# Feed-forward pipeline of a two-layer decoder: transposes moved from TensorE to VectorE and DMAs

## The reference

```
x = layernorm(x + local_attention(x) @ Wo.T + bo)
x = layernorm(x + cross_attention(x, ctx))
# blocks of 16: scale = max|x|/6, rounded to the grid 0, .5, 1, 1.5, 2, 3, 4, 6
gate = q(x) @ q(w_gate).T          # 512 -> 1408
up   = q(x) @ q(w_up).T
h    = silu(gate) * up
x = layernorm(x + q(h) @ q(w_down).T)   # 1408 -> 512
```

## Time and profile before

| | |
|---|---|
| median of 3 runs | 2977.15 us (2976.79 to 2977.43) |
| the profiled execution | 2972.92 us, span 2971.2 us |
| mean granted clock of TensorE | 0.963 |
| PE busy | 2687.5 us, 90% |
| VectorE busy | 1836.1 us, 62% |
| ScalarE busy | 863.2 us, 29% |
| last stage | from about 1728 us to the end |

### The profile page before, as it was taken

How to read it: one execution, slowest core, us unless ns; L and a number is a source line. 1 busy time by engine, 2 the same in 40 slices (tenths; PEclk the granted TensorE clock), 3 DMA queues, 4 the chain that set the end, 5 groups by cost and what they waited for, 6 DMA issues and landing times. The chain is left out here.

```text
span 2971.2 us, 39571 instructions
## 1 busy us (share of the span) xinstructions
PE 2687.5 (90%) x14548; PEld 1389.4 (47%) x14548; DVE 1836.1 (62%) x3454; ACT 863.2 (29%) x1356; POOL 769.2 (26%) x791
## 2 busy tenths in 40 slices
PE   8999588999996999578887859999999999999997
PEld 4444255555553455244444524444444444444443
DVE  4787403666675344277777736777777777777664
ACT  1111122333322333267767601222222222222210
POOL 1232003544552333355555410000000000000000
PEclk9999699999998999799999979999999999999999
DMA  4332510000000233322222420000000000000000
GB/s 169 128 124 86 156 62 1 1 1 1 1 1 32 79 105 98 91 62 79 83 78 80 143 95 11 15 15 14 15 15 15 15 15 15 15 15 15 11 8 11
DMA packets 172110, 146.36 MB, mean 49 GB/s; under 512 B 23784, under 2 KB 136424, under 8 KB 170896
## 3 DMA queue, kind: packets, MB, share of 16 engines
q1 hardware_dynamic: 158264, 131.58, 14.0%
q10 hardware_dynamic: 13656, 12.26, 1.3%
HBM read 91.29 MB, written 52.43 MB: 48 GB/s over the span
## 5 line engine op out<-in xcount | busy, mean ns | idle before, releaser
L2062 PE MATMUL bank<-tiles,tl_HT 128*128 128x512 f32 x704 | 321.4, 598 | 10.6 <-ACT tl_HT L2120 10.6
L2038 PE MATMUL bank<-tiles,tl_XQT 128*128 128x512 f32 (+1 forms) x768 | 322.2, 563 | 0.0
L2043 PE MATMUL bank<-tiles,tl_XQT 128*128 128x512 f32 (+1 forms) x768 | 318.0, 557 | 0.0
L2248 DVE TENSOR_TENSOR tl_HQ<-bank,tl_HQ 128x512 f32<-128x512 f32 (+1 forms) x96 | 62.1, 647 | 282.5 <-PE bank L2043 282.5
L1556 POOL TENSOR_SCALAR_AFFINE_SELECT tiles<-tiles 128x512 f32<-128x512 f32 x256 | 171.3, 673 | 233.4 <-ACT tiles L1729 189.8
L2043 PEld LDWEIGHTS bank<-tiles,tl_XQT 128*128 128x128 f32 x768 | 145.9, 190 | 156.4 <-issue 122.4
L2038 PEld LDWEIGHTS bank<-tiles,tl_XQT 128*128 128x128 f32 x768 | 142.5, 192 | 136.0 <-issue 110.5
L2105 ACT ACTIVATE tl_HQ<-bank 128x512 f32<-128x512 f32 (+1 forms) x96 | 53.9, 562 | 511.2 <-PE bank L2038 511.2
L2062 PEld LDWEIGHTS bank<-tiles,tl_HT 128*128 128x128 f32 x704 | 126.9, 191 | 141.6 <-issue 141.6
L1978 POOL TENSOR_TENSOR tl_rs<-tl_ve,mhalf 128x1 f32<-128x1 f32 x32 | 17.6, 550 | 495.1 <-DVE tl_ve L2178 495.1
L1785 DVE SCALAR_TENSOR_TENSOR tiles<-tiles,bank 128x1024 f32<-128x1024 f32 (+1 forms) x128 | 141.5, 1147 | 2.9 <-PE bank L1638 2.6
(11 more groups left out here) (285 smaller groups left out, 4981.0 us busy)
## 6 DMA issues: line engine op xcount, KB each, us to landing
fp_weights<-ssm_WS ACTq DMA_DIRECT2D x33, 256.0 KB, 2.0
ssm_xT<-in_x_T SPq DMA_DIRECT2D x8, 1024.0 KB, 6.3
X<-in_x SPq DMA_DIRECT2D x8, 1024.0 KB, 8.9
v<-la_VS SPq DMA_DIRECT2D x32, 256.0 KB, 2.3
unit_g<-la_GH SPq DMA_DIRECT2D x32, 256.0 KB, 2.8
unit_gT<-la_GT SPq DMA_DIRECT2D x32, 256.0 KB, 3.2
la_GN<-unit_g SPq DMA_DIRECT2D x128, 64.0 KB, 1.9
la_VN<-v SPq DMA_DIRECT2D x128, 64.0 KB, 1.9
```

What stands on the lines that cost most here:

```text
L2038: mm = e.matmul(bank[(2 * q) % 3][:, 0:w], XQT[n % 2][:, c, :], WgT[q][:, :, c, :], start=(c == 0), stop=(c == C - 1))
L2043: mm = e.matmul(bank[(2 * q + 1) % 3][:, 0:w], XQT[n % 2][:, c, :], WuT[q][:, :, c, :], start=(c == 0), stop=(c == C - 1))
L2062: mm = e.matmul(bank[DOWN][:, :], HT[:, q, :], WdT[:, q, :], start=(q == 0), stop=(q == IC - 1))
```

## The change

No tile is transposed on PE, but for the small weights of the softmax. Instead VectorE's `transpose` turns each 32x32 block of a tile where it stands (`x_turned`, `xq_turned`, `h_turned`), writing with a stride, and sixteen DMAs of 32 partitions each move the blocks to their partitions (`blocks_moved`): those of x all on SP's queue, those of XQ and h half on SP's and half on ScalarE's. The features that land in one chunk are then interleaved: chunk c takes every 4th (or 11th) column of the buffer (`chunk`), and the weights' features are permuted to match, on the host for three matrices and by four loads in place of one for the down weights. On PE `down` is one group of 11 matmuls. ScalarE's three kinds of eviction fall away. The free banks of PSUM go to `LOUT`, `WEIGHTS` and `SCORES`, which had shared. On VectorE `attended_sum` moves to the next slot, `x_quant` goes ahead of `local_sum` and `product(s, 2)`, and POOL's order follows.

```
+def turned(x):
+    return x.rearrange("p (j r q) -> p j q r", j=4, r=32)
...
-                        e.dma_start(k.FW[3 * (u // 3) + UNIT[u % 3]], WS[u % 3][:, :]).then_inc(s_wst[u % 3].sem, 16)
+                        e.dma_start(k.FW[IC * UNIT[u % 3] + u // 3], WS[u % 3][:, :]).then_inc(s_wst[u % 3].sem, 16)
...
+                                for j in range(4):
+                                    e.dma_start(k.tiles[32 * j:32 * j + 32, DOWN_AT:DOWN_AT + IC * D].rearrange("p (i d) -> p i d", d=D),
+                                                down_rows[32 * IC * j:32 * IC * (j + 1), :].rearrange("(i p) d -> p i d", p=32)).then_inc(k.d_wd, 16)
...
-    DOWN, HQT, VOUT, SMALL = 3, 4, 6, 7
+    DOWN, VOUT, WEIGHTS, LOUT, SCORES = 3, 4, 5, 6, 7
...
+        chunk = lambda x, c: x[:, :].rearrange("p (t c) -> p c t", t=P)[:, c, :]
...
+        def blocks_moved(e, token_rows, src, dst, done):
+            w = 32 * (src.shape[1] // P)
+            for i in token_rows:
+                for j in range(4):
+                    e.dma_start(dst[32 * j:32 * j + 32, w * i:w * i + w], src[32 * i:32 * i + 32, w * j:w * j + w]).then_inc(done.sem, 16)
+
+        def h_moved(e, n, token_rows):
+            e.wait_ge(s_ht.sem, s_ht.at(n + 1))
+            e.wait_ge(s_d.sem, s_d.at(n))
+            blocks_moved(e, token_rows, tmp[:, :], HT[:, :], s_hd)
+
+        def xq_moved(e, n, token_rows):
+            e.wait_ge(s_qt.sem, s_qt.at(n + 1))
+            e.wait_ge(s_u.sem, s_u.at(NP * (n - 1)))
+            blocks_moved(e, token_rows, XQB[:, :], XQT[n % 2][:, :], s_qd[n % 2])
+
+        def x_moved(e, n, token_rows):
+            e.wait_ge(s_xt.sem, s_xt.at(n + 1))
+            e.wait_ge(s_s.sem, s_s.at(n))
+            blocks_moved(e, token_rows, XB[:, :], XT[:, :], s_td)
@@ SP, in a slot, after the store of out @@
+                    if there(s - 1):
+                        h_moved(e, s - 1, (0, 1))
+                    if there(s + 1):
+                        xq_moved(e, s + 1, (0, 1))
+                    if there(s + 5):
+                        load_attended(s + 5)
+                    if there(s + 3):
+                        x_moved(e, s + 3, range(4))
@@ PE @@
                 def scores(n):
-                    e.wait_ge(s_tc.sem, s_tc.at(n + 1))
+                    e.wait_ge(s_td.sem, s_td.at(256 * (n + 1)))
+                    e.wait_ge(s_sb.sem, s_sb.at(n))
...
-                        mm = e.matmul(bank[SMALL][:, 0:HM], XT[:, c, :], M2[:, c, b * HM:(b + 1) * HM],
+                        mm = e.matmul(bank[SCORES][:, 0:HM], chunk(XT, c), M2[:, c, b * HM:(b + 1) * HM],
...
+                def down(n):
+                    if n == 0:
+                        e.wait_ge(k.d_wd, 64)
+                    e.wait_ge(s_a6.sem, s_a6.at(n))
+                    e.wait_ge(s_hd.sem, s_hd.at(256 * (n + 1)))
+                    for q in range(IC):
+                        mm = e.matmul(bank[DOWN][:, :], chunk(HT, q), WdT[:, q, :], start=(q == 0), stop=(q == IC - 1))
+                    mm.then_inc(s_d.sem, 1)
@@ PE, order in a slot @@
                     if there(s + 2):
                         transpose_weights(s + 2)
                     if there(s - 1):
-                        transpose_h(s - 1, 0)
-                        transpose_h(s - 1, 1)
-                        down(s - 1, 0)
-                        transpose_h(s - 1, 2)
-                        down(s - 1, 1)
+                        down(s - 1)
                     if there(s + 2):
                         attend(s + 2)
-                    if there(s + 1):
-                        transpose_xq(s + 1)
-                    if there(s - 1):
-                        down(s - 1, 2)
@@ ScalarE, order in a slot @@
                         silu(s, 1)
                     if there(s + 2):
                         exp(s + 2)
+                    if there(s - 1):
+                        h_moved(e, s - 1, (2, 3))
                     if there(s):
                         silu(s, 2)
                     if there(s + 2):
                         copy_weights(s + 2)
...
                     if there(s + 1):
-                        copy_xq(s + 1)
+                        xq_moved(e, s + 1, (2, 3))
@@ VectorE @@
+                def h_turned(n):
+                    e.wait_ge(s_hq.sem, s_hq.at(n + 1))
+                    e.transpose(turned(tmp[:, :]), HQ[n % 2][:, :]).then_inc(s_ht.sem, 1)
...
                     if there(s - 1):
                         h_scaled(s - 1)
+                        h_turned(s - 1)
+                    if there(s + 1):
+                        x_quant(s + 1)
+                        xq_turned(s + 1)
                     if there(s + 3):
                         local_sum(s + 3)
                     if there(s):
                         product(s, 2)
-                    if there(s + 1):
-                        x_quant(s + 1)
                     if there(s + 3):
                         local_normal(s + 3)
+                        x_turned(s + 3)
                     if there(s):
                         h_divide(s)
```

More of the change, by code:

```diff
@@ L1922, in attention_outputs_and_feed_forward @@
         st6, mv6, ve6, rs6 = sb("st6", [P, 6]), [sb(f"mv6{p}", [P, 2]) for p in range(2)], sb("ve6", [P, 1]), sb("rs6", [P, 1])
-        XQ, XQT = sb("XQ", [P, D]), [sb(f"XQT{p}", [P, C, P]) for p in range(2)]
+        XQ, XQT = sb("XQ", [P, D]), [sb(f"XQT{p}", [P, D]) for p in range(2)]
+        XB, XQB = sb("XB", [P, D]), sb("QB", [P, D])
         tmp = sb("tmp", [P, FI])
         HQ = [sb(f"HQ{p}", [P, FI]) for p in range(2)]
-        HT = sb("HT", [P, IC, P])
+        HT = sb("HT", [P, FI])
         am, rs = sb("am", [P, FI // BLK]), sb("rs", [P, FI // BLK])
@@ L1952, in _ @@
                 e.dma_start(MQ[:, :], k.SW[:, M2_AT:VO_AT]).then_inc(s_wm.sem, 16)
[L1953 to L1959, removed]
+                for s in SLOTS:
+                    if there(s - 2):
+                        n = s - 2
+                        e.wait_ge(s_x6.sem, s_x6.at(n + 1))
+                        e.dma_start(k.out[n % B, (n // B) * P:(n // B + 1) * P, :], x_tile(n)).then_inc(s_out.sem, 16)
+                    if there(s - 1):
[6 more added lines that the diff above has]
+                        x_moved(e, s + 3, range(4))
                 e.wait_ge(s_out.sem, s_out.at(16 * NT))
@@ L1988, in local_out @@
                     e.wait_ge(s_at[n % 2].sem, s_at[n % 2].at(16 * (n // 2 + 1)))
-                    e.wait_ge(s_a5.sem, s_a5.at(n - 1))
+                    e.wait_ge(s_a4.sem, s_a4.at(n))
                     for c in range(C):
-                        mm = e.matmul(bank[VOUT][:, :], AT[n % 2][:, c, :], WoT[:, c, :], start=(c == 0), stop=(c == C - 1))
+                        mm = e.matmul(bank[LOUT][:, :], AT[n % 2][:, c, :], WoT[:, c, :], start=(c == 0), stop=(c == C - 1))
                     mm.then_inc(s_lo.sem, 1)
[L1994 to L1999, removed]
                 def scores(n):
@@ L2012, in transpose_weights @@
                     e.wait_ge(s_p.sem, s_p.at(n + 1))
-                    e.matmul(bank[SMALL][rows(n), 0:P], SM[:, :], k.ident[:, :], start=True, stop=True).then_inc(s_pm.sem, 1)
+                    e.wait_ge(s_pc.sem, s_pc.at(n))
+                    e.matmul(bank[WEIGHTS][rows(n), 0:P], SM[:, :], k.ident[:, :], start=True, stop=True).then_inc(s_pm.sem, 1)
                 def attend(n):
@@ L2141, in _ @@
                         copy_weights(s + 2)
-                    if there(s - 1):
-                        for r in range(NR):
-                            copy_h(s - 1, r)
                     if there(s + 1):
-                        copy_xq(s + 1)
+                        xq_moved(e, s + 1, (2, 3))
             @block.vector
@@ L2281, in h_scaled, with x_turned, xq_turned @@
                     e.tensor_tensor(y, y, spread(sc[n % 2][:, :]), ALU.mult).then_inc(s_hq.sem, 1)
+                def x_turned(n):
+                    e.wait_ge(s_x4.sem, s_x4.at(n + 1))
+                    e.wait_ge(s_td.sem, s_td.at(256 * n))
+                    e.transpose(turned(XB[:, :]), x_tile(n)).then_inc(s_xt.sem, 1)
+                def xq_turned(n):
+                    e.wait_ge(s_xq.sem, s_xq.at(n + 1))
+                    e.wait_ge(s_qd[(n - 1) % 2].sem, s_qd[(n - 1) % 2].at(256 * ((n - 1) // 2 + 1)))
+                    e.transpose(turned(XQB[:, :]), XQ[:, :]).then_inc(s_qt.sem, 1)
+                def h_turned(n):
+                    e.wait_ge(s_hq.sem, s_hq.at(n + 1))
+                    e.transpose(turned(tmp[:, :]), HQ[n % 2][:, :]).then_inc(s_ht.sem, 1)
                 for s in SLOTS:
@@ L2354 @@
     arrays |= {n + "_T": np.ascontiguousarray(np.asarray(inputs[n]).T) for n in _TRANSPOSED}
+    for n in ("L1_xattn_Wq", "L1_ffn_w_gate", "L1_ffn_w_up"):
+        arrays[n] = np.ascontiguousarray(np.asarray(inputs[n]).reshape(-1, 4, C, 32).transpose(0, 2, 1, 3).reshape(-1, D))
     ctx = np.asarray(inputs["ctx_1024"])
```

99 lines of the change are left out of this document (28 added, 71 removed).

## The result

The changed kernel takes 3152.23 us (median of 4 runs, 3149.58 to 3153.29) against 2976.97 before on the same chip: 1.0588 times as long, 95% interval 1.057 to 1.0606. I had said 3021 us (2945 to 3115): right in direction, 131 us short in size and outside my range.

What follows compares the result with a forecast made beforehand. PE was taken to bound the kernel in 27 slots of 37.04 us, with latency chains in fill and drain. Fill 27, steady slots 0 and drain 17 gave +44 us on 2977.15: 3021 us, range 2945 to 3115.

Steps and rivals of the forecast that it cites:

- Removed, 2.69 us a slot: PE's transposes of h, XQ and x go, so a slot without new waits takes 34.35 us instead of 37.04.
- VectorE's transposes at the price of a plain pass: Three added transposes on VectorE cost 0.69 us for 512 columns and 1.62 for 1408, 3.0 us a slot.
- Issue at 0.68, landing 1.9 us: Each SBUF-to-SBUF DMA takes its queue 0.68 us from start to start; the last lands 1.9 us after issue.
- rivals with cheap issues: DMA issues on SP and ScalarE cost 0.47 us or less: 2955 us, or 2912 at 0.31; chance 0.31.
- SP as the bound: DMA issues at 0.84 us make scores wait 2.6 us for x each slot: 3133 us; chance 0.12.
- The wait of PE for h, 2.55 us: Before down, PE is ready at +9.05 but may go on at +11.6: a new stall of 2.55 us a slot.
- Nothing, and why: Strided chunk reads, POOL's moved power, new banks and four down-weight DMAs cost 0; weight loads stay covered inside matmuls.
- rival (d): Strided access is slow: scores +0.86, h_turned +1.6, x chain +2.7, about 3 us more a slot, about 3100 us; chance 0.11.
- `down` at 9.43 us after the wait: On PE after the stall for h, 22 down matmuls of 0.43 us take 9.43 us.
- Fill: DMA chains for x and XQ delay the first gate by 23.7 us; slot 2 begins about 27 us later.
- The stage before: The down weights load there in four DMAs, whose landing nobody awaits: 0.
- Drain: Slots 29 to 31 have less cover for h, a stall near 6 us; with the very end together +17 us.

Runs made afterwards that it cites:

- e12: e6 with x, XQ and h all moved in runs of 32 elements, written plainly by VectorE and read contiguously by PE; 2928.43 us (one run).
- e2: The changed kernel with VectorE's three transposes writing their blocks contiguously, features in the wrong order; 3089.5 us (one run).
- e8: The changed kernel with both VectorE's transposes written contiguously and PE's chunks read contiguously, features in the wrong order; 3049.66 us (one run).
- e6: e3 with half of x's DMAs on ScalarE's queue and the down weights loaded in the last stage; 2968.16 us, ratio 0.9972 to the kernel before.
- e4: The changed kernel with four superfluous 128x512 matmuls on PE ahead of down's wait for HT; 3103.65 us (one run).
- e1: The changed kernel with PE reading its chunks of XT, XQT and HT contiguously, features paired with wrong weights; 3144.56 us (one run).
- e3: The changed kernel with h_scaled and h_turned moved ahead of product(s,1) and weights(s+2) on VectorE; 2988.22 us, ratio 1.0047 to the kernel before.
- e5: The changed kernel with the down weights loaded by one DMA instead of four, their rows in another order; 3144.8 us (one run).
- e7: The changed kernel with the edits of e3 and e1 together: h turned early and chunks read contiguously; 2958.07 us (one run).

## Why the prediction was wrong, step by step

**Removed, 2.69 us a slot: right.** e12, with no wait and no stride, has 34.48 where I had 34.35.

**VectorE's transposes at the price of a plain pass: right only for plain writes** (e2: 0.71 and 1.65 us). As written they take 1.08 to 1.10 and 2.70, not the double that I named as the bad case. Of the three only the one for h was on the steady slot's path, with 1.05 us.

**Issue at 0.68, landing 1.9 us: right.** 0.62 to 0.66 and 1.8 to 2.0. This was the number that I took to decide the case, and the rivals with cheap issues and with SP as the bound fall by it. In the steady slots of the changed kernel PE never waits for x. (By the steps that I gave, SP's x would be late by 3.2 us at 0.84, not 2.6, and early by 3.5 at 0.47, not 5; neither price came.)

**The wait of PE for h, 2.55 us: the mechanism right, the term mis-sized** by the strided write, 3.61. e2 shows 2.55 when only that is taken away, and e8 the same.

**"Nothing, and why": wrong for the strided reads.** I argued that up to twice 0.19 us is covered by a matmul's 0.43. Loads of 0.31 to 0.33 us are indeed covered inside a group, but those of scores, whose matmuls are short, are not (1.68 us for 0.84), and a little shows in the first two gates (3.66 for 3.54, 3.61 for 3.49) and in `down` (9.77 in e6, 9.64 in e12). Together 1.21 us, and the mean slots of e6 and e12 differ by 1.22. This was my rival (d), at a chance of 0.11: its scores (+0.86) and the reason were right, its +1.6 for the transpose of h came as 1.05, and its 2.7 us on x never reached PE. Its 3100 us lies nearer to the measured time than my own number, but by that term on x, where the runs show the clock: that is luck. The rule that I quoted there, of the Trainium skill ("SBUF — State Buffer", section "Door 1: The DMA port swizzle"), is borne out: 190 ns of load become 308 to 324 at a step of 16 bytes and 328 at 44 (325 at full clock, e6).

**`down` at 9.43 us after the wait: a step that failed, and that no rival had.** I counted 22 records of 0.43 us, at a clock of 1.00, behind a stall that I had just put there myself. Of this no term of my sum and no rival says anything. After 3.6 us of idle PE the clock falls to its lower level; e4 prices that at 1.70 us a slot (46 over the 27), and e1 shows that it can swallow a real saving nearly whole. The Trainium skill ("TensorE: Matmul & The Clock Gate", section "HAM oscillation — how this bites in real kernels") describes a kernel in which a recurring wait on a DMA makes each burst of matmuls start slow; the trace agrees, with 1.7 us for each wait of 3.6.

The slot put together from the runs: 34.48 (e12) + 1.21 (strided reads) + 3.61 (the wait) + 1.70 (the clock) = 41.00, measured 41.11. The 4.1 us by which it misses my 37.0 are, over 27 slots, 110 of the 136 us by which the span misses my sum.

The terms don't act apart, though, and e8 tells by how much. With both strides gone, the work in the same order and the wait at the 2.55 us of my forecast, the mean slot is 37.54: there the low clock adds only 0.5 us, since it comes in about every third slot. The other 3.6 us of the 4.1 came with the strided accesses: 1.05 by the wait, 1.21 by the reads, and some 1.3 because with the longer wait the clock falls in every slot. So the reads that I put at nothing and the plain price of h's transpose, with the low clock that they bring on, are the larger part of the miss.

**Fill: right to the first gate** (+22.7 for +23.7), 4 us short behind it (+7.3 for +3.3; in e3, without the wait for h, +2.0). **The stage before: wrong**, +7.0 for 0. I wrote that nobody awaits the landing of the four loads; but the stage's last store stands behind them on SP's queue, and the end of the stage awaits that. From the last store's issue to the next stage's first load it took 20.3 us in place of 15.1 (5.2 of the 7.0), and 16.5 with one load (e5); the store itself is issued 1.5 us later, at 1714.00. **Drain: half.** The waits for HT are 7.0, 6.9 and 6.7 us where I had near 6, and 18.5 for the last; but each of the four `down` products takes 11.5 to 12.7 us, where one with strided reads takes 9.8 at full clock, 9 us more in all. It is the clock again: 0.50 in the window 3060 to 3064, 0.70 in 3064 to 3068. Some 7 us of it are part of the missing 16, since before the change the last tile's transposes and products ran at 0.50 too (window 2948 to 2952) and took 13.3 us for the 11.4 of the tile ahead. Up to 4 more are the strided transpose of h, 1.05 us for each of four tiles; the rest stays open.

What stays open is why with the same wait of 2.55 us the clock falls in some slots and not in others (e2 about every second, e8 about every third), and why it stays low longer in e1. Whether fill and drain can be made shorter wasn't tried beyond e6.

## What to carry to other kernels

When a sum puts a stall ahead of a block of matmuls, price the block at the lower clock too: here 3.6 us of waiting cost 5.3, and 2.55 us cost 1.5 to 1.7 more in every second or third slot. Before a transfer replaces work on the bound engine, start its chain as early as its input allows, ahead of everything on that engine that nobody is waiting for yet; that move was worth 164 us, and all that then still lay between the changed kernel and the one before was 13. And what an edit on the bound engine is worth depends on the stall beside it: contiguous reads gave 0.1 us a slot with a stall of 3.6 us (e1), 1.6 with one of 2.55 (from e2 to e8, where the clock then fell less often too) and 1.1 without a wait for h (e7). So judge an edit again when the stall has changed.

## What the runs showed of the hardware

- A float32 weight load of 128x128 takes 190 ns from contiguous columns, 308 to 311 (gates) or 324 (scores) at a step of 4 elements and, for `down`, 325 at a step of 11 at full clock (e6; 328 in the changed kernel, whose clock is lower in part); VectorE's transpose of 128x512 and 128x1408 float32 takes 0.71 and 1.65 us, and 1.1 and 2.70 when it writes with a step of 4 or 11 elements: half as much again or a little more, not double.
- A DMA from SBUF to SBUF over 32 partitions takes 0.62 to 0.66 us of its queue, whether it moves 16 or 44 KB. In runs of 128 bytes those of 16 KB stay there, and those of 44 KB take 0.69 to 0.74 us (e12, where eight fill 5.53 us on SP and 5.90 on ScalarE from 2210.90).
- Runs of 128 bytes cost 0.4 us of landing for h and 0.11 of the DMA engines' time. The Trainium skill ("DMA: Bandwidth & Descriptors", section "Why small descriptors are slow (HBM only)") says that transfers inside SBUF don't suffer the slowness of small descriptors. The trace agrees only in part: nobody had to wait for the 2.3 us in place of 1.9, but for about the same bytes (53 and 50 GB/s) the engines are busy for 0.29 of the time in e12 and 0.18 in e6.
- PE is slower after waiting: 4 superfluous matmuls in the wait of each slot made the kernel 48.6 us faster (e4).
- A store of 128 KB landed 1.7 us after its issue in e6. Issued on the same queue behind the down weights (2.9 MB), it landed after 7.7 us when they went in one load (before) and after 13.0 when they went in four (after).
